# Input products of a gated unit, split into high and low parts, with the scale in the weights and the offset in the bias

## The reference

```python
        xn = (q - mu) / jnp.sqrt(var + EPS) * ln_g + ln_b
        u = jax.nn.silu(xn @ Wu.T + bu)
```

## Time and profile before

| what | value |
|---|---|
| median of 3 runs | 841.31 us (840.61 to 843.43) |
| profiled execution, first to last instruction | 838.9 us |
| what lies around it, as median less span | 2.4 us |
| PE busy | 810.6 us, 97% of the span |
| DVE, POOL, ACT busy | 630.8, 587.2, 473.1 us |

### The profile page before, as it was taken

The page is one execution under the profiler, slowest core; times in us unless marked ns, Lnnn a source line. Parts: engine busy times, 40 slices in busy tenths (PEclk is TensorE's granted clock), DMA queues, the critical chain, the costliest instruction groups (busy, mean ns, idle before and its releaser), DMA issues.

```text
span 838.9 us, 13787 instructions
## 1 busy us (share of the span) xinstructions
PE 810.6 (97%) x5002; PEld 464.7 (55%) x5002; DVE 630.8 (75%) x1041; ACT 473.1 (56%) x849; POOL 587.2 (70%) x385
## 2 busy tenths in 40 slices
PE   6998999999999999999899999999999999999998
PEld 5664454444445444467544444454444444887687
DVE  6997888777778777366877788777777777677773
ACT  3865555555555655768655555555565556654622
POOL 3766668878877887946558888678888877355840
PEclk9999999999999999999999999999999999999999
DMA  6000000000000000000000000000000002200001
GB/s 179 1 2 1 1 1 2 1 1 1 2 1 1 2 1 1 1 1 2 1 1 1 1 1 1 1 1 2 1 1 1 2 1 52 45 10 2 1 1 51
DMA packets 49741, 8.00 MB, mean 10 GB/s; under 512 B 42502, under 2 KB 48266, under 8 KB 49674
## 3 DMA queue, kind: packets, MB, share of 16 engines
q1 hardware_dynamic: 48810, 6.99, 5.3%
q10 hardware_dynamic: 864, 0.13, 0.1%
HBM read 5.92 MB, written 1.05 MB: 8 GB/s over the span
## 4 chain that ended last, share of the span: by engine, by line
PE 80%; DVE 11%; issue 3%; ACT 2%; POOL 2%; DMA 1%; SPq 1%; DVEq 0%; POOLq 0%; ACTq 0%
PE psum L707 26%; PE psum L692 19%; PE psum L672 12%; PE psum L722 4%; DVE part L1236 4%; PE psum L735 3%; PE psum L1811 2%; PE psum L560 2%; PE psum L1838 1%; PE psum L562 1%; PE psum L561 1%; PE psum L1868 1%; DVE space L1252 1%; PE psum L1800 1%; PE psum L653 1%
## 5 line engine op out<-in xcount | busy, mean ns | idle before, releaser
L529 POOL TENSOR_TENSOR space<-space 128x1024 f32<-128x1024 f32 x160 | 380.4, 2378 | 23.7 <-ACT space L956 5.6
L1236 DVE TENSOR_REDUCE part<-psum 128x2 f32<-128x1024 f32 x256 | 313.2, 1224 | 110.6 <-PE psum L672 107.8
L956 ACT ACTIVATE space<-psum 128x512 f32<-128x512 f32 x512 | 264.5, 602 | 144.8 <-PE psum L692 121.5
L707 PE MATMUL psum<-space,vb 128*64 128x512 f32 x1024 | 247.5, 605 | 2.1 <-ACT space L956 2.1
L534 POOL TENSOR_TENSOR space<-space 128x1024 f32<-128x1024 f32 x30 | 71.5, 2385 | 100.3 <-DVE space L1252 100.3
L672 PE MATMUL psum<-kh,qh 64*128 64x512 f32 x512 | 127.4, 494 | 5.8 <-DVE part L1236 4.7
L707 PEld LDWEIGHTS psum<-space,vb 128*64 128x64 f32 x1024 | 62.5, 136 | 108.2 <-issue 71.7
L672 PEld LDWEIGHTS psum<-kh,qh 64*128 64x128 f32 x512 | 47.6, 183 | 132.2 <-DVE part L1236 99.3
L692 PE MATMUL psum<-qh,kh 64*128 64x512 f32 x512 | 103.3, 396 | 0.0
L692 PE MATMUL psum<-ql,kh 64*128 64x512 f32 x512 | 102.0, 390 | 0.0
L692 PE MATMUL psum<-qh,kl 64*128 64x512 f32 x512 | 101.9, 390 | 0.0
(11 more groups left out here) (249 smaller groups left out, 1034.0 us busy)
## 6 DMA issues: line engine op xcount, KB each, us to landing
ql<-nmx SPq DMA_DIRECT2D x256, 0.5 KB, 2.0
wproj<-in_L_ffn_W SPq DMA_DIRECT2D x4, 256.0 KB, 2.9
out<-x SPq DMA_DIRECT2D x3, 256.0 KB, 2.1
x<-in_L_attn_x SPq DMA_DIRECT2D x2, 256.0 KB, 4.4
wproj<-in_L_attn_Wq SPq DMA_DIRECT2D x1, 512.0 KB, 6.6
x<-in_L_attn_x SPq DMA_DIRECT2D x1, 512.0 KB, 7.5
wout<-in_L_attn_Wout SPq DMA_DIRECT2D x1, 512.0 KB, 7.1
w1s<-in_L_ffn_W SPq DMA_DIRECT2D x2, 256.0 KB, 3.1
```

The lines of the kernel that those rows point to most:

```text
L529: pool.tensor_tensor(to, pt[0] if u == 1 else to, pt[u], ALU.add)\
L707: last = pe.matmul(outp[rows(h), :], vb[:, place(m)[1], kt, :], pt[kt][:, h, :], start=(kt == 0), stop=(kt == TILES - 1))
L956: act.activation(pt[kt][:, h, :], key_scores[kt % 2][h], ACT.Exp).then_inc(exp_made, 1)
L1236: dve.tensor_reduce(to[:, half, :], scores.rearrange("p (h k) -> p h k", h=2), AX_X, ALU.max, negate=True)\
```

## The change

Before, ScalarE applied gain and offset when it copied the turned rows, and each block of `gau_in` was one float32 product. Now ScalarE only copies (`in_high`), VectorE subtracts the copy from the turned rows in PSUM (`low_in`, into `in_low`), and each block is three products of float32r: low weights with high rows, high weights with high rows, high weights with low rows. The third product of a block is issued after the first two of the next. The gain goes into the weights: ScalarE makes `in_w` = `wt` times gain between the gelus of chunks 2 and 3 (640 columns), and VectorE the low part in two instructions of 384 and 256 columns (`low_in_weights`), the second into the free columns of `up_high[0]`. The offset goes into the bias: in the first phase of the attention VectorE multiplies the raw weights with the offset row, sums, and adds to `uvb_bias` (`fold_bias`, three instructions); SyncE loads that row with one transfer more. TensorE turns chunk 3's rows after four blocks of chunk 2, not three.

```diff
+        bias_row = vecs[:, 0:2, :].rearrange("p a d -> p (a d)")
+        bias_terms = xnt[:, 0, 0:UVB].rearrange("p (e d) -> p e d", d=P)
+        bias_sums = firsts[:, 0, 0:UVB // P]
...
+            sp.wait_ge(cross_made, 1)
+            sp.dma_start(bias_row, everywhere(a["L1_attn_ln_b"])).then_inc(bias_row_in, 16)
...
+            def fold_bias():
+
+                dve.wait_ge(r_in, 16 * N_RAW)
+                dve.wait_ge(bias_row_in, 16)
+                dve.wait_ge(shared_in, 16 * len(small))
+                dve.tensor_tensor(bias_terms, raw[:, 0:UVB].rearrange("p (e d) -> p e d", d=P), over_mid(bias_row, UVB // P), ALU.mult).then_inc(bias_step, 1)
+                dve.wait_ge(bias_step, 1)
+                dve.tensor_reduce(bias_sums, bias_terms, AX_X, ALU.add).then_inc(bias_step, 1)
+                dve.wait_ge(bias_step, 2)
+                dve.tensor_tensor(c["uvb_bias"][:, :], c["uvb_bias"][:, :], bias_sums, ALU.add).then_inc(c["bias_folded"], 1)
...
+                    if b == 0 and ph == LAG + 1:
+                        fold_bias()
...
-        turned1 = w1s[1].rearrange("p (n a) f -> p n (a f)", n=CHUNKS - EARLY)
+        with ExitStack() as before_unit:
+            w1s = [up_weights(c["wproj"]), sb("w1s", [P, TOP, HID], F32, before_unit)]
+        in_w = mine("in_w", [P, TOP * HID], F32R)
...
+        LOW_HERE = 3
+
+        def in_high_w(e):
+            return in_w[:, e * P:(e + 1) * P]
+
+        def in_low_w(e):
+            return in_w[:, (IN + e) * P:(IN + e + 1) * P] if e < LOW_HERE else up_high[0][:, (2 * HT + e - LOW_HERE) * P:(2 * HT + e - LOW_HERE + 1) * P]
...
-        def turned(ch):
-            return c["xnt"][:, 0, ch * CW:(ch + 1) * CW] if ch < EARLY else turned1[:, ch - EARLY, :]
+        def in_high(ch):
+
+            b, h = batch_half(ch)
+            return row_high[b][:, h * CW:(h + 1) * CW]
+
+        def in_low(ch):
+
+            b, h = batch_half(ch)
+            return row_low[b][:, h * CW:(h + 1) * CW]
...
+                elif n >= ROWS_1:
+                    pe.wait_ge(in_rows_low, n - ROWS_1 + 1)
...
                 pe.wait_ge(rows_kept, ROWS_1 + n + 1)
+                if n == 0:
+                    pe.wait_ge(in_low_made, 2)
                 for e in range(first, end):
                     m = FIRST_IN + n * IN + e
                     wait_wide(pe, m)
-                    pe.matmul(wide(m), wt[:, e * P:(e + 1) * P], turned(ch), start=True, stop=True).then_inc(uvb_made, 1)
+                    pe.matmul(wide(m), in_low_w(e), in_high(ch), start=True, stop=False)
+                    pe.matmul(wide(m), in_high_w(e), in_high(ch), start=False, stop=False)
+                    if e == first + 1:
+                        pe.wait_ge(in_rows_low, n + 1)
+                    if e > first:
+                        pe.matmul(wide(m - 1), in_high_w(e - 1), in_low(ch), start=False, stop=True).then_inc(uvb_made, 1)
+                pe.matmul(wide(m), in_high_w(end - 1), in_low(ch), start=False, stop=True).then_inc(uvb_made, 1)
...
             gau_in(1, 1)
-            gau_in(2, 2, 0, 3)
+            gau_in(2, 2, 0, 4)
             turn(ROWS_1 + 3, 3)
-            gau_in(2, 2, 3, IN)
+            gau_in(2, 2, 4, IN)
...
-                if scale is None:
-                    act.activation(turned(ch), at, ACT.Copy, **({} if total is None else dict(accum_out=total))).then_inc(rows_kept, 1)
-                else:
-                    act.activation(turned(ch), at, ACT.Identity, bias=bias, scale=scale).then_inc(rows_kept, 1)
+                act.activation(in_high(ch), other(OTHER.index(("rows", n))), ACT.Copy).then_inc(rows_kept, 1)
...
-            for ch in range(2, CHUNKS):
-                gelu(ch)
-            keep(ROWS_1, 0, c["lng"][:, 0:1], c["lnb"][:, 0:1])
-            keep(ROWS_1 + 1, 1, c["lng"][:, 0:1], c["lnb"][:, 0:1])
+            gelu(2)
+            act.wait_ge(up_low_made, 2)
+            act.activation(in_w[:, 0:UVB], wt[:, 0:UVB], ACT.Identity, scale=c["lng"][:, 0:1]).then_inc(in_high_made, 1)
+            gelu(3)
+            keep(ROWS_1, 0)
+            keep(ROWS_1 + 1, 1)
+            act.wait_ge(c["bias_folded"], 1)
             silu(0, 0)
-            keep(ROWS_1 + 2, 2, c["lng"][:, 0:1], c["lnb"][:, 0:1])
+            keep(ROWS_1 + 2, 2)
             silu(1, 1)
-            silu(2, 2, 0, 3)
-            keep(ROWS_1 + 3, 3, c["lng"][:, 0:1], c["lnb"][:, 0:1])
-            silu(2, 2, 3, IN)
+            silu(2, 2, 0, 4)
+            keep(ROWS_1 + 3, 3)
+            silu(2, 2, 4, IN)
...
+                if first_wait:
+                    first_wait()
...
+                if second_wait:
+                    second_wait()
...
+            def low_in(n):
+
+                dve.wait_ge(rows_kept, ROWS_1 + n + 1)
+                dve.tensor_tensor(in_low(n), other(OTHER.index(("rows", ROWS_1 + n))), in_high(n).bitcast(F32), ALU.subtract).then_inc(in_rows_low, 1)
+
+            def low_in_first():
+                low_in(0)
+                low_in(1)
+
+            def low_in_third():
+                low_in(2)
+
+            def low_in_weights():
+
+                dve.wait_ge(in_high_made, 1)
+                dve.wait_ge(hid_made, 2 * UP)
+                here = LOW_HERE * P
+                dve.scalar_tensor_tensor(out=in_w[:, UVB:UVB + here], in0=wt[:, 0:here], scalar=c["lng"][:, 0:1], in1=in_w[:, 0:here].bitcast(F32),
+                                         op0=ALU.mult, op1=ALU.subtract).then_inc(in_low_made, 1)
+                dve.scalar_tensor_tensor(out=up_high[0][:, 2 * HT * P:2 * HT * P + UVB - here], in0=wt[:, here:UVB], scalar=c["lng"][:, 0:1],
+                                         in1=in_w[:, here:UVB].bitcast(F32), op0=ALU.mult, op1=ALU.subtract).then_inc(in_low_made, 1)
...
-            after_ffn(1)
+            after_ffn(1, first_wait=low_in_weights)
             for ch in (2, 3):
                 add_bias(ch)
             dve.wait_ge(b2_added, CHUNKS)
-            after_ffn(2)
-            after_ffn(3)
+            after_ffn(2, second_wait=low_in_first)
+            after_ffn(3, second_wait=low_in_third)
             products(0, 0)
+            low_in(3)
```

13 lines of the change are left out of this document (8 added, 5 removed).

## The result

| what | before | after |
|---|---|---|
| median (6 runs each) | 841.47 us (840.61 to 843.43) | 845.26 us (844.10 to 846.54) |
| profiled execution, first to last instruction | 838.9 us | 844.7 us |
| ratio of times | | 1.0036 [1.0022, 1.0051] |

What follows compares the result with a forecast made beforehand. TensorE, busy 97% of the span, was taken to bound the kernel, with ScalarE setting the unit's last block. Terms 2.4 + 0.8 - 1.7 = +1.5 us on 838.9 gave 840.4, with 2.4 around it 842.8, given as 842.7; range 840.2 to 845.3.

Steps and rivals of the forecast that it cites:

- the same: Whole kernel: a time of 838.8 to 843.8 us, which a measurement can't tell from no change; chance 0.70.
- Term 3: Attention's first phase: GpSimd holds VectorE's small bias addition, so the maximum is late and TensorE waits; cost 2.4 us.
- the 1.15 forecast for that case: Bias in the attention: if GpSimd doesn't hold the small addition, cost 1.15 us; rival with nothing held anywhere, chance 0.17.
- a rival on the clock: Behind the narrow products of `gau_dots`: the clock fall there may vanish (841.2 us) or come twice (844.2); chance 0.13 in all.
- Term 2: Ahead of the unit: VectorE's low weights hold up GpSimd before an awaited root; cost 0.8 us, bounds 0 and 0.9.
- Term 1: Unit's input products: cheaper split products start `turn_position` earlier; gain 1.7 us, bounds 0.6 and 3.4.
- the walk through the stage on the old clock: Unit: step by step on the old times, `turn_position` starts at 783.95 instead of 785.66, gain 1.7 us.
- The stall of 0.5 us for the low rows of chunk 2: Unit: TensorE wants these rows at 774.7, VectorE has them ready at 775.2.
- The 2.4 us that lie around the span: Outside first to last instruction: 2.4 us added to the forecast span of 840.4 us to give 842.8.
- may come twice: Clock rival, behind `gau_dots`: the fall costing 1.5 us comes twice, giving 844.2 us; chance 0.13 with its other half.
- a gain if the fall vanishes: Clock rival, behind `gau_dots`: without the fall 1.5 us less, 841.2 us; chance 0.13 with its other half.

Runs made afterwards that it cites:

- e3: Changed kernel with the bias's third instruction a sum over five single columns (one SBUF operand) instead of the two-operand addition; 842.84 us, ratio 1.0003.
- e6: Changed kernel with the three bias instructions spread over three following attention phases, one each; 842.11 us, ratio 0.9998.
- e4: Kernel before plus only the offset row's transfer, the three bias instructions and ScalarE's wait for them; 844.4 us, ratio 1.003.
- e5: Changed kernel with the two low parts of the weights made one normalisation later, in chunk 2's; 843.8 us, ratio 1.0014.
- e1: Changed kernel without the three bias instructions, the first silu keeping a second, long satisfied wait; 841.07 us, ratio 0.9986.
- e9: Changed kernel with the edits of e2 and e6, the low weights staying where the change put them; 841.2 us, ratio 0.9982.
- e2: Changed kernel with ScalarE's wait for the folded bias moved from the first silu to before its pass over the weights; 843.55 us, ratio 1.0021.
- e10: e9 with ScalarE taking the first silu of chunk 3 between the second and third of the first four heads; 840.25 us, ratio 0.998.
- e7: Changed kernel with the edits of e2, e5 and e6 together; 841.76 us, ratio 0.9991.
- e8: Changed kernel without the bias instructions and any wait for them, low weights made in chunk 2's normalisation; 840.95 us, ratio 0.9992.

## Why the prediction was right or wrong

The forecast of 842.7 us lies 2.6 us under the median, inside the range of 840.2 to 845.3 by a hair. Of the three outcomes it gave most to "the same" (0.70) and 0.25 to slower; the ratio of 1.0036 is on the slower side of 0.3%, though its interval reaches below that. That the median still falls inside the range is partly luck: of the 3.8 us between the medians the terms give about half, and the prediction prices nothing that would give the rest in the likeliest case.

**Term 3, the bias: right in mechanism and size, and incomplete.** Forecast 2.4 us, with the small addition held until GpSimd's addition ends; measured 2.15 us, of which the addition alone took 1.35. It started at 78.28, the maximum at 79.55, where the working had 78.5 and 80.0. `e3` and `e6` show the hold as the cause, and the 0.97 us that is left in `e3` without it lies below the 1.15 forecast for that case. What the step left out is what TensorE does after a stall: in the profiled execution its clock fell to 0.69 and the next two units lost 1.36 us. The prediction had a rival on the clock, but only for the place where the trace of before showed a fall; that a new stall may bring a new fall was priced nowhere. `e4` shows that it need not come.

**Term 2, the low weights: right in mechanism, and smaller.** Forecast 0.8 us, bounds 0 and 0.9. The hold is 0.58 us (`e5`), although the two low parts took 0.62 and 0.49 us and not 0.54 and 0.40; the turn came 0.89 us later in the changed kernel, 0.6 in `e1`, 0.53 in `e9`, and 0.00 in `e5`, which has the low weights elsewhere. That 0.89 is so near the forecast is luck: 0.3 of it is VectorE's late start against TensorE, which no term has. Which of GpSimd's instructions was held was wrong: the four products ahead of the addition (2.64 us against 2.01), not the addition, which kept its 1.27.

**Term 1, the products: mis-sized, 0.97 us instead of 1.7.** The failed step is the walk through the stage on the old clock. It took the table load to stand where it stood, in ScalarE's idle time. With the added wait it stands behind the first block, and 1.28 us of load came between that block and its silu, of which 0.74 us reached TensorE. ("ScalarE's copies get no dearer" held: two took 1.08 us, against 1.45.) `e2` undoes exactly this and measures 1.71 us. What was late next, ScalarE with the heads, was named rightly (wait of 1.3 us, and `e10` removes it). The stall of 0.5 us for the low rows of chunk 2 did not occur in the changed kernel, since TensorE was held up by the late table; it appears, as 0.53 and 0.56 us, in `e7` and `e8`. In `e2` and `e9` there is none. In every version with the split products TensorE waits 0.46 to 0.48 us for ScalarE's copy of chunk 3's rows, which the walk doesn't have. Nor does TensorE alone give back 3.4 us but 2.6, for the first product behind a turn or a wait takes 0.31 to 0.34 us to the next one, not 0.23. That 1.7 fits `e2` so well is partly luck.

**The base.** "The 2.4 us that lie around the span" were 2.24 for the kernel before, 1.8 for the kernels with the split products (1.9 for `e8`) and 2.1 for `e4`. That is 0.4 to 0.6 us in the changed kernel's favour that no term has, and I have no cause for it.

**The sum.** The three terms as measured give 2.15 + 0.89 - 0.97 = +2.1 us, not +1.5. Between the medians the spans differ by 3.8 + 0.4 = 4.2 us. The other 2.1 us I put down to clock falls: the median run of the changed kernel has a clock of 0.994, while the commonest of the kernel before are 0.996 and 0.998. That split is argued, not shown. Among runs of one clock the changed kernel's span is 1.65 us longer (0.996) and 1.2 us longer (0.994), less than the terms give. And the six runs of the kernel before were quick ones: the 90 later ones have medians about 1.1 us higher. One such fall stands behind the stall. The others come in the second half of the unit: from the first `turn_position` to the gated products the profiles have 20.65 us with no fall (`e2`), 20.22 with one (before, `e6`; 20.67 in `e8`, 21.58 in `e4`, where it came early, ahead of the second `turn_position`), and 21.84 to 21.96 with two or one long one (changed kernel, `e1`, `e3`, `e5`, `e7`, `e9`, `e10`). So the prediction's rival "may come twice" came in the profiled execution, at 1.6 us where it had 1.5. Its other half, a gain if the fall vanishes, isn't seen in the one profile without a fall there (`e2`): VectorE is late instead. What decides between one fall and two wasn't found, and is left open. The 90 runs of the kernel before at 0.994, 0.996, 0.998 and 1.000 have median spans of 842.4, 840.7, 839.2 and 839.0 us: the first step down costs 0.2 us, as far as five runs at 1.000 can tell, and each further one 1.5 to 1.7.

## What to carry to other kernels

A second wait, though long satisfied, cost time here because it stood on the first instruction that needs another activation table: the load then came only when the last of the two waits ended. Put a long satisfied semaphore's wait on an earlier instruction, and read the order with its waits, not only the order.

Small work for an engine with thin slack goes in pieces, one to a phase, and an instruction with two SBUF operands goes where GpSimd is idle: the same three instructions stalled TensorE for 2.1 us together and not at all apart. Before such work is placed, compare its length with the slack of one phase (here 0.5 us behind a gap of 0.4), not with the busy share of the engine, which was 75%.

When a stage is made faster, look at which engine ends it. Here TensorE's last wait in the unit was for one silu behind four heads, and changing their order gave 1.0 us.

## What was not expected of the hardware

- A stall of TensorE of 2.08 us was followed by a granted clock of 0.69 over 5.5 us in three of four profiled executions that had it (changed kernel, `e2` with 0.68, `e5` with 0.69), and by 1.00 in the fourth (`e4`). The level within it is 1.2 GHz instead of 2.4: a product's record goes from 0.39 to 0.63 us. After the stall of 0.88 us in `e3` the clock stayed up, and no profile without a stall has a fall there. The Trainium skill, page TensorE: Matmul & The Clock Gate, section What's actually happening, says that the gate follows how busy TensorE has been lately and that it knows two levels. The rows agree on the two levels; `e4` shows that a stall of this length doesn't by itself decide on a fall.
- What a fall of the clock costs goes by where it lies. Behind the second `turn_position` one of 3.4 us only takes away a wait for VectorE (20.22 us with it, 20.65 without any), while one of about 8 us costs as much as two (`e5`, 21.85). Between the two `turn_position` it makes that stretch 1.6 us longer (10.52 against 8.90); in `e4`, which has this one alone, 0.7 us come back behind it, since 21.58 us in all stand against 20.65.
- The table load took 1.28 us and the activations behind it started 1.30 us after its start. The Trainium skill, page ScalarE: Activation LUTs, section What ACT_TABLE_LOAD costs, has 1.283 us for the load, which agrees, and 1.38 us more for a drain; behind an idle ScalarE, at 773.24, no such time is to be seen.
